# Three projections moved in a Perceiver-style kernel: queries' rows made by TensorE, late value products spread, a third chunk's values projected in the delta rule's front

## The chip, the cores and the metric

The kernel runs on one core of a Trainium2 chip. The core has five engines with queues of their own: TensorE (PE), VectorE (DVE), ScalarE (ACT), GpSimd (POOL) and SyncE (SP), which issues DMAs. They meet only through semaphores. PE writes to eight PSUM banks of 128 x 512 fp32, which DVE and ACT read. The metric is the device time in microseconds (us) of one execution.

## The reference

An input x of 128 rows x 256 passes through two layers; both attend to the same context of 12544 rows x 256.

```python
# layer 0: 4 heads of 64, softmax over 12544 context rows
x = x + softmax((ln(x) Wq)(ctx Wk)^T / 8) (ctx Wv) Wo
x = x + gated_delta_net(ln(x))        # 12 heads, 128 steps, short convolutions
x = x + moe(ln(x))                    # 8 experts, best 1
# layer 1: 16 heads of 16, softmax over the same context rows
x = x + softmax((ln(x) Wq' + bq)(ctx Wk' + bk)^T / 4) (ctx Wv' + bv)
x = x + gated_decay_attention(ln(x))
x = x + moe(ln(x))                    # 8 experts, best 2
```

## The kernel before

The context is cut into `NCH` = 14 chunks of 896 rows (seven tiles of 128). **Layer 0** streams them. DVE turns a chunk (`turn_context`, four steps T0 to T3), PE makes layer 0's keys (K0 to K3), layer 1's keys (J0 to J3) and both layers' values (V0 to V6, 512 columns: 256 for each layer), scores (S0 to S7), turned exponentials and value products. `PLAN0` is the order by hand; in a step chunk c's products stand between the projections of c + 1. Layer 1's keys go to DRAM (`kscr`) as six bf16 terms made by POOL, its values (`v1s`) to `vscr`. From chunk `LATE` = 12 on, layer 1's values are left out (256 columns); the turned context of these chunks stays in `ctxT0` and `ctxL`. A Fori loop runs steps 1 to 10. `PRO0` is the order of chunk 0's projections; in it "W0" turns the layer-1 weights (six DVE transposes, four on PE), which J0 needs.

**The delta rule** follows. Its front is serial: layer 0's output `o0`, its product with Wo, layer norm, gates, short convolutions, decay sums (`below`, L1194), norms (L1149). `spin` issues products of the identity whose results nobody reads. `vp` holds the products of the convolution taps.

**The experts**, then **layer 1**. `second_vector` splits the queries into three bf16 parts (`q3`). `qrows` needs them as 96 rows, six terms (`Q_TERM`) of 16 dimensions, heads side by side. SP writes `q3` to DRAM (`qscr`) and reads it back in six pieces. Then PE walks the prologue `PRO1`: 16 heads' scores of chunk 0, one of chunk 1, "M" (the turned running maximum, L1717), seven more of chunk 1. Two pairs of banks alternate, so a head's scores wait for the maximum (DVE, L1849) of the head two before. `late_values` makes the missing layer-1 values of chunks 12 and 13, five double units before the scores and two among them; ACT copies them to slots 1 and 2 of `v1`, SP stores them, and then fetches chunks 1 and 2 into these slots. POOL fills the three last rows of the keys (L1671, 3 x 12288 and 3 x 9216) and the matrix `blk16`, then takes up `maximum(c)`, whose result "M" turns. After that the chunks are streamed: transposed scores (L1752), exponentials (ACT), value products (L1765).

## Time and profile before

| what | value |
|---|---|
| runs | 1026.24, 1027.66, 1031.89 us (median 1027.66) |
| profiled execution | 1026.65 us, its span 1024.9 us, mean granted clock 0.99 |
| busy share of the span | PE 95%, weight loads 59%, ACT 52%, DVE 48%, POOL 29% |
| layer 0 / delta rule / experts | 0 to 517.7 / to 621.0 / to 638.3 us |
| layer 1's front / its streamed chunks | to 684.2 / to about 990 us |
| late values in layer 1's front | 28 products |

Times in the rows are microseconds from the span's start; a row of the timeline gives start, length, engine, line, operation, output and inputs with their form, the number of instructions, and in brackets the idle time before and who ended it. An fp32 product of PE counts as two records. A stage's limit is read from the brackets of the engine that is waited for.

### The profile page before, as it was taken

What the parts mean: (1) busy time and instruction counts of PE and PEld (TensorE: products, weight loads), DVE (VectorE), ACT (ScalarE), POOL (GpSimd) and SP (SyncE); (2) the same over time, 40 slices, a digit from 0 to 9 for tenths busy, and PEclk for the clock granted to TensorE, in tenths of its full rate; (3) what the DMA queues carried; (4) which work ended last, traced back from release to release, by engine and by line L of the source; (5) the groups of instructions that cost most, each with busy time, mean ns of one, the idle gap of its engine ahead of it and who ended that gap; (6) DMA issues with size and microseconds to landing.
All of it is one profiled execution on the core that took longest, in us unless ns stands there. A gap on an engine that the chain in (4) does not pass through costs nothing. (4 is left out here: it accounts for less than half of the span.)

```text
span 1024.9 us, 22398 instructions
## 1 busy us (share of the span) xinstructions
PE 973.8 (95%) x8646; PEld 608.7 (59%) x8646; DVE 494.1 (48%) x1002; ACT 535.8 (52%) x1243; POOL 301.8 (29%) x428
## 2 busy tenths in 40 slices
PE   8999999999999999999988998889999999999987
PEld 4445454554454554455577995647666666666775
DVE  3224233232332423333254453488878777887526
ACT  2544544454454454445547622226666666666753
POOL 5444253443344425344503611700100000010000
PEclk9999999999999999999999999989999999999999
DMA  9456646636546462552200005777657677765200
GB/s 157 159 154 189 184 169 181 156 116 135 130 160 171 126 186 104 124 151 108 76 34 1 2 1 151 178 214 226 154 151 182 171 172 185 183 157 151 86 3 5
DMA packets 106067, 136.88 MB, mean 134 GB/s; under 512 B 66568, under 2 KB 87840, under 8 KB 103296
## 3 DMA queue, kind: packets, MB, share of 16 engines
q1 hardware_dynamic: 102272, 134.81, 48.2%
q10 hardware_dynamic: 3712, 0.92, 0.6%
q8 instruction: 58, 0.95, 0.4%
q14 instruction: 25, 0.20, 0.1%
HBM read 81.88 MB, written 53.26 MB: 132 GB/s over the span
## 5 line engine op out<-in xcount | busy, mean ns | idle before, releaser
L1849 DVE TENSOR_REDUCE mx<-bank 128x1 f32<-128x896 f32 x224 | 233.8, 1086 | 62.3 <-PE bank L1709 58.9
L1910 ACT ACTIVATE p<-bank 128x512 f32<-128x512 f32 x392 | 204.0, 602 | 105.2 <-PE bank L1752 105.1
L549 PE MATMUL bank<-Wv,ctxT 128*128 128x512 f32 (+1 forms) x364 | 164.6, 587 | 0.0
L1752 PE MATMUL bank<-qrows,krows 99*128 99x128 bf16 x1568 | 124.4, 220 | 7.1 <-ACT p L1910 4.6
L1709 PE MATMUL bank<-krows,qrows 96*128 96x512 bf16 x448 | 125.3, 363 | 5.8 <-DVE mx L1849 4.8
L1752 PEld LDWEIGHTS bank<-qrows,krows 99*128 99x128 bf16 x1568 | 99.3, 97 | 44.5 <-issue 11.0
L618 DVE CUSTOM_DVE_ANT_0 sc<-bank,pen 128x448 f32<-128x448 f32 x112 | 65.7, 620 | 116.5 <-issue 116.5
L1765 PE MATMUL bank<-p,v 128*32 128x128 f32 x3136 | 108.4, 276 | 3.9 <-issue 3.9
L432 POOL CAST kt<-kf 128x512 bf16<-128x512 f32 (+1 forms) x56 | 31.1, 556 | 271.2 <-ACT kf L711 271.2
L1765 PEld LDWEIGHTS bank<-p,v 128*32 128x32 f32 x3136 | 80.6, 109 | 39.0 <-ACT p L1910 31.4
L549 PEld LDWEIGHTS bank<-Wv,ctxT 128*128 128x128 f32 x364 | 65.0, 190 | 64.2 <-issue 59.3
L529 PE MATMUL bank<-ctxT,WTk 128*128 128x512 f32 (+1 forms) x208 | 88.4, 547 | 1.0 <-ACT v L718 0.6
L1649 POOL TENSOR_SCALAR neg<-run 128x16 f32<-128x16 f32 x14 | 3.6, 255 | 274.5 <-DVE run L1864 274.5
L513 PE MATMUL bank<-ctxT,Wk 128*128 128x448 f32 x208 | 82.6, 540 | 1.2 <-issue 1.2
L726 ACT COPY v<-bank 128x256 f32<-128x256 f32 x84 | 31.1, 371 | 99.8 <-PE bank L549 99.8
L747 ACT COPY pT<-bank 128x512 f32<-128x512 f32 x98 | 56.6, 583 | 47.5 <-PE bank L560 47.4
L739 ACT ACTIVATE sc<-sc,neg 128x448 f32<-128x448 f32 x112 | 73.5, 663 | 0.2
L711 ACT ACTIVATE kf<-bank,b 128x512 f32<-128x512 f32 (+1 forms) x56 | 35.5, 634 | 69.7 <-PE bank L529 69.7
L560 PEld LDWEIGHTS bank<-ident,sc 128*128 128x128 f32 x392 | 42.8, 140 | 40.1 <-issue 32.5
L560 PE MATMUL bank<-ident,sc 128*128 128x128 f32 x392 | 62.3, 282 | 4.1 <-ACT pT L747 1.5
L644 DVE COPY ots<-bank 128x256 f32<-128x256 f32 x14 | 5.9, 425 | 124.5 <-PE bank L572 124.5
L434 POOL TENSOR_TENSOR kt<-kf,kt 128x512 bf16<-128x512 f32 (+1 forms) x56 | 61.4, 1096 | 4.5
(303 smaller groups left out, 1267.1 us busy)
## 6 DMA issues: line engine op xcount, KB each, us to landing
krows<-kscr SPq DMA_DIRECT2D x14, 1536.0 KB, 10.1
krows<-kscr SPq DMA_DIRECT2D x14, 1152.0 KB, 14.4
v<-vscr SPq DMA_DIRECT2D x14, 1004.5 KB, 12.7
vscr<-v1s SPq DMA_DIRECT2D x12, 1004.5 KB, 3.9
kscr<-kt SPq DMA_DIRECT2D x14, 768.0 KB, 3.6
kscr<-kt SPq DMA_DIRECT2D x14, 576.0 KB, 3.0
kscr<-kt SPq DMA_DIRECT2D x14, 512.0 KB, 4.5
ctxB<-ctx SPq DMA_DIRECT2D x56, 112.0 KB, 3.6
```

The lines of the kernel that those rows point to most:

```text
L434: pool.tensor_tensor(kh[:, 1, b], f, kh[:, 0, b], ALU.subtract).then_inc(S("k21"), 1)
L513: ins = pe.matmul(bank[kv_bank(op, s)][:, 0:HCH], Wk0[:, i, b * P:(b + 1) * P], turned_context(c)[:, i, half * HCH:(half + 1) * HCH], star ...
L529: ins = pe.matmul(bank[kv_bank(op, s)][:, 0:HW[half]], WTk[:, i, b * P:(b + 1) * P], turned_context(c)[:, i, HO[half]:HO[half] + HW[half]] ...
L549: ins = pe.matmul(bank[kv_bank(op, s)][:, 0:w * D], turned_context(c)[:, i, k * P:(k + 1) * P], Wv01[:, i, 0:w].rearrange("p w o -> p (w o)"),
L560: ins = pe.transpose(bank[PT[(s + t) % 2]][:, h * P:(h + 1) * P], sc0[:, s, h, t * P:(t + 1) * P], ident[:])
L618: dve.tensor_tensor_reduce(out=sc0[:, s, h, half * HCH:(half + 1) * HCH], in0=bank[SX[k % 2]][:, 0:HCH], in1=pen0[:, half * HCH:(half + 1) ...
L739: act.activation(sc0[:, s, h, cols], sc0[:, s, h, cols], ACT.Exp, bias=neg0[:, h:h + 1], accum_out=den0[:, s, h, half:half + 1]).then_inc( ...
L1709: ins = pe.matmul(bank[b + half][:, 0:HW[half]], qrows[0:KROWS, 0, h, :], krows[half][0:KROWS, r, krow(h), :], start=True, stop=True)
L1752: ins = pe.matmul(bank[ST1[g % 3]][:, i * P:(i + 1) * P], krows[half][:, c % R1, krow(h), cols], qrows[:, c % 2, h, :], start=True, stop=True)
L1765: ins = pe.matmul(bank[OT1][32 * i:32 * i + 32, j * P:(j + 1) * P], v1[:, c % R1, t, h * (D1 + 1):h * (D1 + 1) + 32], p1[:, g % PR, i * P: ...
L1849: dve.tensor_reduce(mx1[:, c % 2, h:h + 1], psum[:, b:b + 2, :].rearrange("p b n -> p (b n)")[:, 0:CH], AX.X, ALU.max).then_inc(S("smread1 ...
L1910: act.activation(p1[:, g % PR, :], bank[ST1[g % 3]][:], ACT.Exp).then_inc(S("exp1"), 1)
```

## The change

Chunk 11 joins the late chunks (`LATE` = 11). Chunk 12's turned context goes to `ctxM`, the upper part of `vpair`, a buffer that outlives layer 0 and serves as `v1s` before and as `vp` after. Its layer-1 values are made in the delta rule's front (`mid_values`, seven units of two products) and stored by SP; POOL clears `vp` after that. Chunks 11 and 13 are made in layer 1, 14 single units, one before the scores and 13 among them (`LAFTER`).

The queries' rows are made by PE: `picks` holds columns of the identity, written by POOL during the experts into `v1`'s slot 2; 24 products (`pick_rows`) give the 96 rows of 16 heads, and ACT copies them in four pieces. The gather of chunk 1's keys is issued ahead of that.

In layer 0's start SP waits for the first half of chunk 0's context ahead of the layer-1 weights, and "W0" stands behind the first two scores. The Fori loop runs steps 1 to 8, and 9 and 10 stand in straight code.

```diff
@@ -176,7 +176,7 @@
-        LATE = NCH - 2
+        LATE = NCH - 3
@@ -188,6 +188,7 @@
+        vpair = sb(gw, "vpair", [P, TAPS * 2 * GH * P])
@@ -250,7 +251,8 @@
-        v1s = sb(l0, "v1s", [P, 2, CT, VW])
+        v1s = vpair[:, 0:2 * CT * VW].rearrange("p (s t w) -> p s t w", s=2, t=CT)
+        ctxM = vpair[:, CT * VW:CT * VW + DC * CH].rearrange("p (i m) -> p i m", i=DC)
@@ -268,7 +270,7 @@
-        PRO0 = ALL0[0:8] + ("W0",) + ALL0[8:]
+        PRO0 = ALL0[0:10] + ("W0",) + ALL0[10:]
@@ -289,7 +291,9 @@
-            return ctxL if isinstance(c, int) and c == NCH - 1 else ctxT0
+            if isinstance(c, int) and c >= NCH - 2:
+                return ctxL if c == NCH - 1 else ctxM
+            return ctxT0
@@ -298,8 +302,10 @@
+                elif turned_context(c) is ctxL:
+                    dve.wait_ge(S("ctxT0"), 4 * c)
...
-                    dve.wait_ge(S("ctxT0"), 4 * c)
+                    dve.wait_ge(S("vscr_1"), 16 * (LATE // 2))
@@ -376,11 +382,11 @@
-            with eng.Fori(0, (NCH - 4) // 2) as i:
+            with eng.Fori(0, (NCH - 6) // 2) as i:
...
-            step(NCH - 3, 1, (NCH - 4) // 2)
-            step(NCH - 2, 0, (NCH - 2) // 2)
+            for c in range(NCH - 5, NCH - 1):
+                step(c, c % 2, c // 2)
@@ -463,6 +469,7 @@
+                sp.wait_ge(S("ctx0_0_0"), 64)
                 for k, name in ((1, "L1_xattn_Wk"), (2, "L1_xattn_Wv"), (0, "L1_xattn_Wq")):
@@ -824,16 +832,26 @@
+        MIDBANK = ((5, 0), (4, 0), (4, D), (5, 0), (7, 0), (7, D), (6, 0))
         def even_odd(tile, g):
...
         with nc.Block() as block:
+            @block.sync
+            def _(sp):
+                sp.wait_ge(S("v1mid"), CT)
+                sp.dma_start(vscr[NCH - 2].rearrange("p t w -> p (t w)"),
+                             v1s[:, 0].rearrange("p t w -> p (t w)")).then_inc(S("vscr_mid"), 16)
+                sp.wait_ge(S("vscr_mid"), 16)
             @block.gpsimd
...
+                pool.wait_ge(S("vscr_mid"), 16)
                 for j in range(TAPS - 1):
@@ -1046,8 +1064,18 @@
+                def take_mid(t, n):
+                    b, o = MIDBANK[t]
+                    act.wait_ge(S("v1mid_psum"), t + n)
+                    act.copy(v1s[:, 0, t:t + n, 0:H1 * (D1 + 1)].rearrange("p t (h d) -> p t h d", h=H1)[:, :, :, 0:D1],
+                             bank[b][:, o:o + n * D].rearrange("p (t h d) -> p t h d", t=n, h=H1)).then_inc(S("v1mid"), n)
+                take_mid(0, 1)
...
+                take_mid(1, 2)
+                take_mid(3, 1)
@@ -1060,6 +1088,9 @@
                 keep_rows(3)
+                act.activation(spare0[:], mhalf[:, 0:1], ACT.Silu)
+                take_mid(4, 2)
+                take_mid(6, 1)
                 silu(0, "conv", 1)
@@ -1169,7 +1200,20 @@
-                spin(pe, 5, 5)
+                def mid_values(t):
+                    b, o = MIDBANK[t]
+                    if t == 3:
+                        pe.wait_ge(S("v1mid"), 1)
+                    if t == 4:
+                        pe.wait_ge(S("gstep"), 1)
+                    for k in range(DC):
+                        ins = pe.matmul(bank[b][:, o:o + D], ctxM[:, k, t * P:(t + 1) * P], Wv01[:, k, 1, :],
+                                        start=(k == 0), stop=(k == DC - 1))
+                    ins.then_inc(S("v1mid_psum"), 1)
+                mid_values(0)
+                spin(pe, 4, 2)
                 pe.wait_ge(S("o0"), 1)
@@ -1179,9 +1223,10 @@
                 ins.then_inc(S("x1_psum"), 1)
-                spin(pe, 5, 11)
+                for t in range(1, 4):
+                    mid_values(t)
                 ln_pe(pe, "ln1", 7)
-                spin(pe, 5, 2)
+                spin(pe, 3, 2)
                 pe.wait_ge(S("ln1_hT"), 1)
@@ -1189,13 +1234,17 @@
                     project(g)
+                for t in range(4, CT):
+                    mid_values(t)
                 pe.wait_ge(S("R"), 1)
                 for g in range(NG):
+                    if g == 2:
+                        pe.wait_ge(S("v1mid"), CT)
                     pe.matmul(bank[DB[g]][:], below[:], R[:, hb(g)].rearrange("p h t -> p (h t)"), start=True,
...
                 pe.wait_ge(S("qcopy"), 2)
-                spin(pe, 2, 14)
+                spin(pe, 2, 5)
                 pe.wait_ge(S("sq"), 1)
@@ -1500,7 +1549,9 @@
-        qscr = nc.dram_tensor("qscr", (3, D, P), BF16).ap()
+        HB = P // D1
+        pickhome = v1[:, 2].rearrange("p t w -> p (t w)")[:, 0:3 * HB * KROWS // 2]
+        picks = pickhome.bitcast(BF16).rearrange("p (l k r) -> p l k r", l=HB, k=3)
@@ -1534,15 +1585,22 @@
...
+            value_ones(pool, 1)
+        def value_ones(pool, r):
+            pool.memset(v1[:, r, :, 0:H1 * (D1 + 1)].rearrange("p t (h d) -> p t h d", h=H1)[:, :, :, D1],
+                        1.0).then_inc(S("v1late_ones"), 1)
+            pool.memset(v1[:, r, :, H1 * (D1 + 1):], 0.0).then_inc(S("v1late_ones"), 1)
...
-        LU = 2 * CT // 2
-        LBANK = (4, 5)
+        LATES = (LATE, NCH - 1)
+        LU = 2 * CT
+        LBANK = (4, 5, 7)
+        LAFTER = (0, 1, 3, 4, 6, 7, 9, 10, 12, 13, 15, 18, 20)
+        LATE_FIRST = 1 + sum(1 for n in LAFTER if n <= H1 + 1)
+        NPICK = 4
+        PBANK = (3, 6, 7, 0)
@@ -1607,27 +1665,24 @@
-            sp.wait_ge(S("q3"), 3)
-            sp.dma_start(qscr.rearrange("k (b p) q -> p (k b) q", b=DC),
-                         q3[:].rearrange("p k b q -> p (k b) q")).then_inc(S("qscr"), 16)
-            sp.wait_ge(S("qscr"), 16)
-            for j in range(NJ):
-                sp.dma_start(qrows[j * D1:(j + 1) * D1, 0],
-                             qscr[Q_TERM[j]].rearrange("(h d) q -> d h q", d=D1)).then_inc(S("qrows_in"), 16)
-            sp.wait_ge(S("qrows_in"), 16 * NJ)
-            sp.dma_start(qrows[0:KROWS, 1], qrows[0:KROWS, 0]).then_inc(S("qrows_copy"), 16)
...
-            sp.wait_ge(S("v1late"), LU)
-            for r in (1, 2):
-                sp.dma_start(vscr[LATE + r - 1].rearrange("p t w -> p (t w)"),
-                             v1[:, r].rearrange("p t w -> p (t w)")).then_inc(S("vscr_late"), 16)
+            sp.wait_ge(S("qpicked"), NPICK)
+            sp.dma_start(qrows[0:KROWS, 1], qrows[0:KROWS, 0]).then_inc(S("qrows_copy"), 16)
+            def store_late(r):
+                sp.wait_ge(S("v1late"), r * CT)
+                sp.dma_start(vscr[LATES[r - 1]].rearrange("p t w -> p (t w)"),
+                             v1[:, r].rearrange("p t w -> p (t w)")).then_inc(S(f"vscr_late{r}"), 16)
+            store_late(1)
...
-            sp.wait_ge(S("vscr_late"), 32)
-            fetch_values(sp, 1)
-            fetch_values(sp, 2)
+            store_late(2)
+            for r in (1, 2):
+                sp.wait_ge(S(f"vscr_late{r}"), 16)
+                fetch_values(sp, r)
@@ -1641,6 +1696,15 @@
+        def make_picks(pool):
+            pool.wait_ge(S("moe0wt"), 1)
+            pool.memset(pickhome, 0.0).then_inc(S("picks"), 1)
+            pool.wait_ge(S("picks"), 1)
+            for j in range(NJ):
+                pool.tensor_copy(picks[:, :, Q_TERM[j], j * D1:(j + 1) * D1],
+                                 identb[:].rearrange("p (l d) -> p l d", d=D1)).then_inc(S("picks"), 1)
@@ -1665,7 +1729,11 @@
+            make_picks(pool)
             ln_pool(pool, "ln2")
+            pool.wait_ge(S("qpick_psum"), NPICK)
+            value_ones(pool, 2)
+            pool.wait_ge(S("v1late_ones"), 4)
             pool.wait_ge(S("q3"), 3)
@@ -1786,28 +1854,37 @@
...
-                for j in range(2):
-                    r, t = divmod(2 * i + j, CT)
-                    for k in range(DC):
-                        ins = pe.matmul(bank[b][:, j * D:(j + 1) * D], (ctxT0, ctxL)[r][:, k, t * P:(t + 1) * P],
-                                        Wv01[:, k, 1, :], start=(k == 0), stop=(k == DC - 1))
+                b = LBANK[i % 3]
+                if i >= 3:
+                    pe.wait_ge(S("v1late"), i - 2)
+                r, t = divmod(i, CT)
+                for k in range(DC):
+                    ins = pe.matmul(bank[b][:, 0:D], (ctxT0, ctxL)[r][:, k, t * P:(t + 1) * P],
+                                    Wv01[:, k, 1, :], start=(k == 0), stop=(k == DC - 1))
...
-            for i in range(LU - 2):
-                late_values(i)
-            pe.wait_ge(S("qrows_in"), 16 * NJ)
+            def pick_rows(i):
+                pe.wait_ge(S("lT"), (0, 1, 2, 3)[i])
+                for l in range(2):
+                    for k in range(3):
+                        ins = pe.matmul(bank[PBANK[i]][0:KROWS, l * D:(l + 1) * D], picks[:, 2 * i + l, k, :],
+                                        q3[:, k].rearrange("p b q -> p (b q)"), start=(k == 0), stop=(k == 2))
+                ins.then_inc(S("qpick_psum"), 1)
+            pe.wait_ge(S("picks"), NJ + 1)
+            pe.wait_ge(S("q3"), 3)
+            for i in range(NPICK):
+                pick_rows(i)
+            late_values(0)
...
+            pe.wait_ge(S("qpicked"), NPICK)
...
-                if n >= len(PRO1) - 6:
-                    spin(pe, OT1, 2)
-                if n in (3, 7):
-                    late_values(LU - 2 + n // 4)
+                if n in LAFTER:
+                    late_values(LAFTER.index(n) + 1)
+                elif n > len(PRO1) - 7:
+                    spin(pe, 6, 2)
@@ -1914,14 +1991,25 @@
-            act.wait_ge(S("v1late_ones"), 4)
-            for i in range(LU):
+            for i in range(NPICK):
+                act.wait_ge(S("qpick_psum"), i + 1)
+                act.copy(qrows[0:KROWS, 0].rearrange("r (b l) q -> r l b q", b=DC)[:, 2 * i:2 * i + 2],
+                         bank[PBANK[i]][0:KROWS].rearrange("r (l b q) -> r l b q", l=2, b=DC)).then_inc(S("qpicked"), 1)
+            def take_late(i):
+                if i % CT == 0:
+                    act.wait_ge(S("v1late_ones"), 2 * (i // CT) + 2)
+                act.copy(v1late[:, i, 0:H1 * (D1 + 1)].rearrange("p (h d) -> p h d", h=H1)[:, :, 0:D1],
+                         bank[LBANK[i % 3]][:, 0:D].rearrange("p (h d) -> p h d", h=H1)).then_inc(S("v1late"), 1)
+            for i in range(LATE_FIRST):
+                take_late(i)
...
+            for i in range(LATE_FIRST, LU):
+                take_late(i)
```

On DVE at the start (`gate` and `sc` belong to a head's scores) the rows before are:

```order
L345 TENSOR_SCALAR q<-bank 128x256
L663 TENSOR_SCALAR pen<-mask 128x896
L628 STREAM_TRANSPOSE WTk<-v 128x8x16 x2
L631 STREAM_TRANSPOSE Wv<-v 128x256
L628 STREAM_TRANSPOSE WTk<-v 128x8x16 x2
L631 STREAM_TRANSPOSE Wv<-v 128x256
L617 MEMSET gate 128x1
```

and after:

```order
L351 TENSOR_SCALAR q<-bank 128x256
L670 TENSOR_SCALAR pen<-mask 128x896
L624 MEMSET gate 128x1
L625 ISA sc,mx<-bank,pen 128x448
L625 ISA mx 128x1
L624 MEMSET gate 128x1
L625 ISA sc,mx<-bank,pen 128x448
L625 ISA mx 128x1
L635 STREAM_TRANSPOSE WTk<-v 128x8x16 x2
```

Two heads' scores have moved ahead of the six turns. On PE the delta rule's front stood before with spins around the products of `o` (layer 0's output), `xn` (the norm) and `Wc` (convolution inputs):

```order
L163 MATMUL bank<-ident 128x128 x5
L1175 MATMUL bank<-ident,o 128x128 x2
L1180 MATMUL bank<-Wo,oT 128x256 x2
L163 MATMUL bank<-ident 128x128 x11
L157 MATMUL bank<-ident,xn 128x128 x2
```

and stands after with value products of chunk 12 (`vpair`):

```order
L1211 MATMUL bank<-Wv,vpair 128x256 x2
L163 MATMUL bank<-ident 128x128 x2
L1219 MATMUL bank<-ident,o 128x128 x2
L1224 MATMUL bank<-Wo,oT 128x256 x2
L1211 MATMUL bank<-Wv,vpair 128x256 x6
L157 MATMUL bank<-ident,xn 128x128 x2
```

Fourteen of the spins have become four units of value products. On POOL in layer 1, before, the norm's root stood right ahead of the memsets of the keys' rows:

```order
L151 TENSOR_TENSOR rstd<-rstd,mhalf 128x1
L1671 MEMSET krows 3x12288
L1671 MEMSET krows 3x9216
L1674 MEMSET blk 128x128
L1677 AFFINE_SELECT blk<-blk 128x128
```

and after, the clearing of `v1`'s slot 2 (for which POOL waits on `qpick_psum`) stands between:

```order
L151 TENSOR_TENSOR rstd<-rstd,mhalf 128x1
L1591 MEMSET v 128x7x16
L1593 MEMSET v 128x7x15
L1739 MEMSET krows 3x12288
L1739 MEMSET krows 3x9216
L1742 MEMSET blk 128x128
```

The large memsets have moved behind the last product of the picks.

## Rows read from the trace of the kernel before

**Rows 1.** The page, part 5: an ACT copy of one bank

```profile
L747 ACT COPY pT<-bank 128x512 f32<-128x512 f32 x98 | 56.6, 583 | 47.5 <-PE bank L560 47.4
```

**Rows 2.** Timeline, DVE: layer 0's copies (start us, us, engine, line, operation, [idle before])

```profile
403.82 0.42 DVE L644 COPY ots<-bank 128x256 f32<-128x256 f32 x1 [9.48 <-PE bank L572]
...
440.26 0.42 DVE L644 COPY ots<-bank 128x256 f32<-128x256 f32 x1 [9.37 <-PE bank L572]
...
472.65 0.42 DVE L644 COPY ots<-bank 128x256 f32<-128x256 f32 x1 [6.02 <-PE bank L572]
...
504.11 0.42 DVE L644 COPY ots<-bank 128x256 f32<-128x256 f32 x1 [6.01 <-PE bank L572]
```

**Rows 3.** Timeline of the start: context, weight turns, scores, first product J0

```profile
13.04 1.17 DVE L304 STREAM_TRANSPOSE ctxT<-ctxA 128x448 f32<-128x448 f32 x2 [3.81 <-DMA ctxA<-ctx]
...
14.31 3.25 PE L513 MATMUL bank<-ctxT,Wk 128*128 128x448 f32 x8 [1.20 <-issue]
...
15.31 0.65 DVE L628 STREAM_TRANSPOSE WTk<-v 128x128 f32<-128x128 f32 x2 [0.27 <-DMA v<-L_xattn_Wq]
...
16.58 0.41 DVE L631 STREAM_TRANSPOSE Wv<-v 128x256 f32<-128x256 f32 x1
...
17.92 1.02 PE L540 MATMUL bank<-kT,q 64*128 64x448 f32 x4
...
18.88 1.98 PE L529 MATMUL bank<-ctxT,WTk 128*128 128x512 f32 x4
...
18.98 0.62 DVE L618 CUSTOM_DVE_ANT_0 sc<-bank,pen 128x448 f32<-128x448 f32 x1 [1.99 <-issue]
```

**Rows 4.** Timeline of the delta rule's front, PE

```profile
520.93 2.62 PE L163 MATMUL bank<-ident 128*128 128x128 f32 x22
...
533.63 3.29 PE L163 MATMUL bank<-ident 128*128 128x128 f32 x28
...
537.46 1.50 PE L1149 MATMUL bank<-half,sq 128*128 128x2 f32 x12 [0.54 <-DVE sq L926]
```

**Rows 5.** Timeline of layer 1's front, PE, DVE and POOL

```profile
645.21 6.21 PE L1797 MATMUL bank<-Wv,ctxT 128*128 128x256 f32 x28
...
645.67 18.16 POOL L1671 MEMSET krows<- 3x12288 f32 x2 [5.11 <-DVE q L1843]
...
654.81 0.93 PE L1709 MATMUL bank<-krows,qrows 96*128 96x512 bf16 x4 [0.79 <-DMA qrows<-qscr]
...
655.49 4.20 DVE L1849 TENSOR_REDUCE mx<-bank 128x1 f32<-128x896 f32 x4 [9.95 <-PE bank L1709]
...
658.36 2.80 PE L1797 MATMUL bank<-Wv,ctxA 128*128 128x256 f32 x8
...
661.58 4.08 DVE L1849 TENSOR_REDUCE mx<-bank 128x1 f32<-128x896 f32 x4 [1.88 <-PE bank L1709]
...
664.60 0.34 POOL L1680 TENSOR_SCALAR_AFFINE_SELECT blk<-blk 128x128 f32<-128x128 f32 x1
...
672.67 0.93 PE L1709 MATMUL bank<-krows,qrows 96*128 96x512 bf16 x2 [0.19 <-DVE mx L1849]
...
674.76 0.17 DVE L1864 TENSOR_TENSOR run<-run,mx 128x16 f32<-128x16 f32 x1
...
676.51 0.34 PE L1717 MATMUL bank<-identb,n 128*96 128x128 bf16 x1 [1.85 <-POOL n L1661]
...
684.20 0.84 PE L1752 MATMUL bank<-qrows,krows 99*128 99x128 bf16 x12
```

**Rows 6.** Windows: PE busy, granted clock, DMA share, GB/s

```profile
657.00:658.00 1.00, 0.83 (x3) 0.50 1.10 377
...
674.00:675.00 1.00, 0.66 (x2) 0.50 0.06 24
```

**Rows 7.** DMA issues, 626 to 631: KB each, us to landing

```profile
krows<-kscr SPq DMA_DIRECT2D x1, 1536.0 KB, 15.7
krows<-kscr SPq DMA_DIRECT2D x1, 1152.0 KB, 19.9
```

18 lines of the change are left out of this document (4 added, 14 removed).

## The prediction

> **What bounds the kernel now.** I read the page first: TensorE (PE) is busy 95% of the span, but in stages with different limits. I cut the time into stages with the timeline and, inside each, looked at what ends PE's idle time.
>
> In layer 0 the DVE copy that closes a chunk's value product marks the period. The last three gaps are 36.44, 32.39 and 31.46 us [rows 2]. The reader should see that the periods get shorter exactly where a chunk is built without the second half of its value product, so what PE streams there is the bound.
>
> The first chunk's prologue is a mixture. DVE waits 3.81 us for the second half of the context and starts turning it at 13.04; PE starts the key products for it at 14.31, the first scores at 17.92 and the first product J0 at 18.88 [rows 3].
>
> The front of the delta rule is a serial chain through DVE, ACT and POOL. PE fills its waits with empty products (spins) there: 22 and 28 records [rows 4].
>
> The front of layer 1 has two limits in a row. First the round trip of the queries through DRAM: the first scores start at 654.81 with "DMA qrows<-qscr" as releaser. Then DVE's maxima, 1.05 us each (4.20 for four), 24 of them in the prologue, with pauses of which the one at 661.58 (1.88 us, released by PE) is the largest [rows 5]. The streamed chunks after 684.20 do not change.
>
> **The change part by part.** The sum is made against the profiled execution: span 1024.9, its own time 1026.65, which is 1.0 below the median shown (1027.66).
>
> *Layer 0, chunk 11 without the layer-1 half.* Fourteen products get 256 instead of 512 columns, ACT loses seven copies, and SP one store. No need to price them singly: the steps that build chunks 12 and 13 in this way are in the trace. Before, the last three gaps add to 36.44 + 32.39 + 31.46 = 100.29; after, the first short gap moves one chunk forward and a second 31.46 follows: 32.39 + 31.46 + 31.46 = 95.31. Gain 5.0. Bounds: 4.0 (36.44 - 32.39, if the added step got nothing beyond the first short one) to 6.0 (fourteen times the 0.43 that 256 fp32 columns cost, two records of 0.222 each, 6.21 for 28 [rows 5]). Chunk 12's turning no longer waits for chunk 11's last product, but PE was not waiting for it, so that is 0. Two more steps out of the loop are 0 as well: the gap that lies in straight code differs from the looped ones only by its work.
>
> *The start.* Three loads of layer-1 weights now wait until the first half of chunk 0's context is in, and DVE and PE take the first two scores before they turn those weights. The second half of the context should come earlier: DVE was waiting for it since about 9.2, and it shared the DMA with these loads. If it is turned by 13.1, where PE ends the first key products, the second key products start 1.2 earlier, at 13.1. They last 3.25, so the scores start at 16.4. DVE takes them 1.06 after PE begins (17.92 to 18.98), needs 1.17 for two, and only then turns the weights, which took from 15.31 to 16.99 = 1.68. J0 needs all six turns: 16.4 + 1.06 + 1.17 + 1.68 + 0.2 = 20.5 against 18.88 [rows 3]. What was hidden under the wait for the context is now in the chain: a loss of 1.6. Bounds: 2.9 if the context comes no earlier, 0.5 if PE starts the chunk 1.1 earlier too. Behind J0 the prologue is PE's, so the loss is kept.
>
> *Delta rule.* Seven units of two products, 0.89 us each (four records of 0.222, rows 5), 6.2 in all; 23 spins go, 46 records of about 0.118 [rows 4], 5.4. Units 0 to 3 take the places of 14 spins in waits for DVE and POOL. Units 4 to 6 (2.7) stand before the decay sums, and nine spins fewer (2.1) behind them; the next norm product at 537.46 waits for DVE either way. I take 0.15 lost. ACT's four copies fall in its waits, the Silu table is loaded where it was. The new 1 MB store is waited for by POOL alone, whose next work is at 547. If that cover were gone the price would be the whole 6.2; below, it could gain nothing, since spins are not on the path.
>
> *Layer 1, queries by PE.* The qscr write, six reads and the wait go. Instead PE makes 24 bf16 products of 256 columns; no such row exists. The nearest is the bf16 score pair: four matmuls, 1792 columns, in 0.93, so 0.13 for 256 and 3.2 for all; from above, 0.222 each like an fp32 record, 5.3; from below, 2.6, if they run a fifth faster than that pair. I take 3.2. The queries' last part is there when POOL starts at 645.67, so the products end at 648.9; ACT's last copy takes 0.58 [rows 1]; the scores start at 649.5 instead of 654.81. POOL makes the picking tables before, in its idle time during the experts; the first late unit fits beside ACT's copy.
>
> *The score prologue.* The late products (14 units instead of 7 double ones) are spread: PE needs per three heads 3 x 0.46 (half of 0.93) + 2 x 0.89 = 3.16, DVE 3 x 1.05 = 3.15. That is even, with no reserve. I give it 0.5 of friction. First maximum at 650.2, sixteen end at 650.2 + 16.8 + 0.5 = 667.5, against 674.76 [rows 5]. That would be 7.3 earlier.
>
> *But POOL is late next.* Its 18.16 us of memsets on the key rows' tail started at 645.67. Now they stand behind the last pick product and two small memsets, at about 649.5, and end at 667.7; the block matrix behind them ended 1.1 later (664.94 for 663.83), so POOL is free at 668.8, 1.3 after the maximum. From the running maximum to the product that turns it (L1717) are 1.75; from POOL's start 1.5. It comes at 670.3 instead of 676.51: 6.2 earlier. Behind it, 7.69 passed until the streamed scores (684.20). Two late units now stand there in place of two spins: at half clock 1.40 instead of 0.94 each (8 records in 2.80, rows 5; a spin pair is four records of 0.235), so about 1.0 more. Streamed scores at 679.0: gain 5.2. Bounds: 2.5 with PE slower throughout that stretch, 9 if neither POOL nor the clock costs anything and the picks are quick.
>
> GpSimd's work beside DVE has a rule. DVE's maxima take 1.05 each beside POOL's memset (655.49) [rows 5]. The Trainium skill, GPSIMD Engine Reference, section Key points, says that GpSimd shares its SBUF interfaces with VectorE and contends with instructions that have two SBUF inputs. By it, the picks would slow the experts' last DVE steps by up to their own length, some 2 us; no run here shows them, and the sum with them would be 1020.5.
>
> *Sum:* -5.0 + 1.6 + 0.15 - 5.2 = -8.45. 1026.65 - 8.45 = 1018.2; a median that lies a little above a single run makes it 1018.5.
>
> **Rivals.**
> 1. *Nothing else is late* (POOL's memsets and the clock cost nothing). The front gains 8 to 9, the upper bound above: 1015. For it: DVE alone set the pace. Against it: POOL's row is 18.16 long and starts later by construction.
> 2. *PE stays at half clock behind the running maximum.* PE has no work there from about 666.9 to 670.3. The granted clock was 0.50 at 657 and again at 674, each time after PE had done little for some us [rows 6]. Then seven score pairs of 0.93, two late units of 1.40 and four spin pairs of 0.94 make 13.1, against the 8.7 used above: 4.4 more, 1023.
> The Trainium skill (TensorE: Matmul & The Clock Gate, section HAM oscillation) describes this: a gap in PE's work gives the slow clock at the next burst. The trace agrees with the direction.
> 3. *The keys come later, so nothing starts earlier.* Chunk 1's keys are now asked for right behind chunk 0's values. Chunk 0's keys landed 15.7 and 19.9 after their issue at 626.1 and 626.7, so at 646.6, only 2.9 before they are wanted [rows 7]. If both gathers share the engines instead of following one another, 2.65 MB at the same rate (11 us for that size) push it to 657.6 and the front's gain is gone, and more: 1018.5 + 8.1 = 1026.6. Against it: the landings before follow the order of issue.
> 4. *Slower: the spread value products at half clock.* Place: the prologue from the first score to the streamed ones. Price: 24 pairs of 0.93 + 13 units of 1.40 + four spin pairs of 0.94 = 44.3, against 29.5 (649.5 to 679.0): 14.8 more, 1033.3. It decides as soon as the granted clock reads 0.50 for most of 650 to 666; it breaks even with before when it holds for some 60% of it. For it: balance without reserve, and before it fell to half at 657. Against: that followed a wait which is removed, and at full clock PE is never idle for long.
>
> **How the numbers follow.** Forecast 0.56, rival 1 0.14, rival 2 0.15, rival 3 0.08, rival 4 0.05; 0.02 for anything else, slower. The forecast's own range is 1016 to 1021 (terms: start +-1.2, layer 0 +-0.7, front +-1.8). For 8 in 10 I take in rival 1 and rival 2: 1013.5 to 1023.5. A measurement of this kernel tells about 0.5% (5.1 us) from no change, so faster means below 1022.5. Forecast nearly whole, rival 1 and a third of rival 2 are faster: 0.78. Same: two thirds of rival 2, most of rival 3: 0.16. Slower 0.06.
>
> **What the profile after would show.** Layer 0: the copies' last three gaps 32.4, 31.5, 31.5. Start: J0 about 1.6 later, DVE's weight turns behind two scores, and the second context half landing by 11. Delta: the norm product at the same distance from the block's start within 0.3. Layer 1, counted from the first transposes of lraw at 643.03: first scores after 6.5 instead of 11.8; no pause over 0.5 in the first sixteen maxima; POOL's first running-maximum step released by POOL's own work, not by DVE; streamed scores after 36 instead of 41.2. I am wrong if the first scores have a DMA as releaser, if PE's clock reads 0.50 before the sixteenth maximum, if delta grows by more than 1, or if J0 is not later.

## The result and the profile after

| | before | after |
|---|---|---|
| first comparison, median | 1028.38 us (1026.24 to 1031.89, 4 runs) | 1017.33 us (1016.64 to 1017.38, 4 runs) |
| with the runs made beside the experiments | 1028.8 us (1023.7 to 1036.4, 47 runs) | 1016.7 us (1013.1 to 1018.3, 10 runs) |
| profiled execution, its span | 1026.65, 1024.9 | 1017.3, 1015.5 |

The ratio of the first comparison is 0.988, 95% interval 0.9858 to 0.9902. The forecast was 1018.5. It was 9.2 us below the median of 1027.66 that was known then; the medians of the first row differ by 11.0 us, those of the second by 12.1. So the gain was forecast 2 to 3 us too small, while the time itself came out near.

In layer 0 these are the DVE copies that close a chunk's value product, now on line L651 (timeline, DVE). Their gaps are 32.32, 31.46 and 31.47, where before they were 36.44, 32.39 and 31.46 [rows 2].

```profile
404.32 0.42 DVE L651 COPY ots<-bank 128x256 f32<-128x256 f32 x1 [9.37 <-PE bank L579]
436.64 0.42 DVE L651 COPY ots<-bank 128x256 f32<-128x256 f32 x1 [6.02 <-PE bank L579]
468.10 0.42 DVE L651 COPY ots<-bank 128x256 f32<-128x256 f32 x1 [6.02 <-PE bank L579]
499.57 0.42 DVE L651 COPY ots<-bank 128x256 f32<-128x256 f32 x1 [6.02 <-PE bank L579]
```

At the start (timeline, DVE and PE) the second half of the context comes at 10.89 instead of 13.04 and the key products run unbroken. Then J0 (L536) waits 2.40 us for the weight turn on L638, which stands behind two scores, and starts at 19.44 instead of 18.88 [rows 3]. DVE had been idle for 3.52 us ahead of the first score.

```profile
9.33 6.18 PE L520 MATMUL bank<-ctxT,Wk 128*128 128x448 f32 x16
10.89 1.17 DVE L310 STREAM_TRANSPOSE ctxT<-ctxA 128x448 f32<-128x448 f32 x2 [2.12 <-DMA ctxA<-ctx]
15.44 1.02 PE L547 MATMUL bank<-kT,q 64*128 64x448 f32 x4
16.58 0.06 DVE L624 MEMSET gate<- 128x1 f32 x1 [3.52 <-PE bank L547]
18.98 0.41 DVE L638 STREAM_TRANSPOSE Wv<-v 128x256 f32<-128x256 f32 x1
19.44 1.98 PE L536 MATMUL bank<-ctxT,WTk 128*128 128x512 f32 x4 [2.40 <-DVE Wv L638]
```

In the front of the delta rule (timeline, PE) value products (L1211) stand where the empty products stood [rows 4]. The norm product (L1180) comes 19.33 us behind the block's first DVE instruction (513.24 to 532.57; before 517.78 to 537.46, 19.68).

```profile
516.43 2.75 PE L1211 MATMUL bank<-Wv,vpair 128*128 128x256 f32 x12
...
526.16 2.75 PE L1211 MATMUL bank<-Wv,vpair 128*128 128x256 f32 x12
...
531.33 1.28 PE L163 MATMUL bank<-ident 128*128 128x128 f32 x10
532.57 1.50 PE L1180 MATMUL bank<-half,sq 128*128 128x2 f32 x12
```

In layer 1's front (timeline, all engines) the 24 pick products take 2.79, ACT's four copies end at 642.5, and yet the first scores (L1777) wait 1.95 for the keys of chunk 0. Against [rows 5] the scores come 8.23 behind the transposes of lraw (L1852) instead of 11.78, the last update of the running maximum (L1941) 19.31 behind them instead of 19.95, and the streamed scores (L1820) 8.64 behind the turned maximum (L1785) instead of 7.69.

```profile
636.44 2.35 PE L1852 MATMUL bank<-ident,lraw 128*128 128x128 f32 x20
639.06 2.79 PE L1871 MATMUL bank<-q,v 128*96 128x256 bf16 x24 [0.27 <-issue]
639.92 2.55 ACT L1996 CAST qrows<-bank 96x512 bf16<-96x512 f32 x4 [0.30 <-PE bank L1871]
642.41 10.33 POOL L1739 MEMSET krows<- 3x12288 f32 x1
644.67 0.54 PE L1777 MATMUL bank<-krows,qrows 96*128 96x512 bf16 x2 [1.95 <-DMA krows<-kscr]
645.34 1.09 DVE L1926 TENSOR_REDUCE mx<-bank 128x1 f32<-128x896 f32 x1 [6.38 <-PE bank L1777]
647.01 1.09 DVE L1926 TENSOR_REDUCE mx<-bank 128x1 f32<-128x896 f32 x1 [0.58 <-PE bank L1777]
649.41 3.09 DVE L1926 TENSOR_REDUCE mx<-bank 128x1 f32<-128x896 f32 x3 [1.31 <-PE bank L1777]
...
663.98 0.17 DVE L1941 TENSOR_TENSOR run<-run,mx 128x16 f32<-128x16 f32 x1
664.25 0.28 POOL L1713 TENSOR_SCALAR neg<-run 128x16 f32<-128x16 f32 x1 [2.56 <-DVE run L1941]
665.74 0.26 PE L1785 MATMUL bank<-identb,n 128*96 128x128 bf16 x1 [2.10 <-POOL n L1725]
...
674.38 0.84 PE L1820 MATMUL bank<-qrows,krows 99*128 99x128 bf16 x12
```

The granted clock (windows: PE busy, clock, DMA share, GB/s) is 0.50 in two places of that stretch, where it was so at 657 and about 674 before [rows 6]. It is full in the experts.

```profile
621.00:625.00 4.00, 3.92 (x21) 1.00 0.63 192
646.00:649.00 3.00, 3.00 (x9) 0.50 0.95 175
667.00:669.00 2.00, 2.00 (x7) 0.50 0.04 6
```

The experts were not part of the forecast, and they took 14.94 us after and 16.69 before. One product of four records there shows the difference. The first row is from the trace before, the second from the one after:

```profile
627.47 2.88 PE L1326 MATMUL bank<-p,hT 128*128 128x512 f32 x4
```

```profile
621.55 1.88 PE L1375 MATMUL bank<-p,hT 128*128 128x512 f32 x4
```

By stage, from one trace of each: start +0.56, layer 0 behind J0 -5.11, front of the delta rule -0.34, experts -1.75, layer 1 from lraw to the streamed scores -3.23 (41.17 to 37.94), streamed chunks and the end +0.42. That is -9.45, and the spans differ by 9.4. Three of these terms were not forecast in that size: the experts (nothing forecast), the front (-5.2) and the start (+1.6). Their errors cancel in part, so the sum came near the forecast partly by luck. The experiments ask which terms hold in every execution.

### The profile page after: what moved, and what is told of

Read it like the earlier page. It is cut to its first block and busy times, and to the rows that moved or that the text cites. A ratio compares the mean times of both kernels' runs of the same rounds, so it can differ in the third digit from the quotient of the medians.

```text
span 1015.5 us, 22296 instructions
## 1 busy us (share of the span) xinstructions
PE 966.8 (95%) x8648; PEld 609.8 (60%) x8648; DVE 494.1 (49%) x1002; ACT 540.1 (53%) x1253; POOL 304.6 (30%) x435
## 5 line engine op out<-in xcount | busy, mean ns | idle before, releaser
L556 PE MATMUL bank<-Wv,ctxT 128*128 128x512 f32 (+1 forms) x336 | 151.4, 586 | 0.0
L1820 PE MATMUL bank<-qrows,krows 99*128 99x128 bf16 x1568 | 124.6, 220 | 9.3 <-ACT p L1987 4.6
L1820 PEld LDWEIGHTS bank<-qrows,krows 99*128 99x128 bf16 x1568 | 99.2, 97 | 46.4 <-issue 13.1
L1777 PE MATMUL bank<-krows,qrows 96*128 96x512 bf16 x448 | 123.6, 357 | 3.4 <-DMA krows<-kscr 2.0
L556 PEld LDWEIGHTS bank<-Wv,ctxT 128*128 128x128 f32 x336 | 60.0, 190 | 59.1 <-issue 54.5
L536 PE MATMUL bank<-ctxT,WTk 128*128 128x512 f32 (+1 forms) x192 | 81.6, 547 | 3.4 <-DVE Wv L638 2.4
L733 ACT COPY v<-bank 128x256 f32<-128x256 f32 x77 | 28.5, 371 | 91.4 <-PE bank L556 91.4
L520 PE MATMUL bank<-ctxT,Wk 128*128 128x448 f32 x192 | 76.0, 539 | 0.0
L651 DVE COPY ots<-bank 128x256 f32<-128x256 f32 x14 | 5.9, 425 | 121.0 <-PE bank L579 121.0
```

Of the source, the lines that this page charges most:

```text
L520: ins = pe.matmul(bank[kv_bank(op, s)][:, 0:HCH], Wk0[:, i, b * P:(b + 1) * P], turned_context(c)[:, i, half * HCH:(half + 1) * HCH], star ...
L536: ins = pe.matmul(bank[kv_bank(op, s)][:, 0:HW[half]], WTk[:, i, b * P:(b + 1) * P], turned_context(c)[:, i, HO[half]:HO[half] + HW[half]] ...
L556: ins = pe.matmul(bank[kv_bank(op, s)][:, 0:w * D], turned_context(c)[:, i, k * P:(k + 1) * P], Wv01[:, i, 0:w].rearrange("p w o -> p (w o)"),
L1777: ins = pe.matmul(bank[b + half][:, 0:HW[half]], qrows[0:KROWS, 0, h, :], krows[half][0:KROWS, r, krow(h), :], start=True, stop=True)
L1820: ins = pe.matmul(bank[ST1[g % 3]][:, i * P:(i + 1) * P], krows[half][:, c % R1, krow(h), cols], qrows[:, c % 2, h, :], start=True, stop=True)
```

## The experiments

Ten edited kernels ran, and the two of the comparison once more; each also gave a trace. The table has what all traces say of the same stretches, each read from the starts of the timeline's rows. "Last copy" is the last DVE copy of layer 0, "experts" goes to their bias product, "maximum" the last update of the running maximum, "turned" the product that turns it, "streamed" the first transposed scores. The column "half" adds, over one-microsecond windows, twice what the granted clock lacks to 1.00: the time at half clock. A constant 5.3 us between that product and the transposes of lraw is left out.

| kernel | J0 at | to last copy | to experts | experts | lraw to scores | to maximum | to turned | to streamed | to end | half | span |
|---|---|---|---|---|---|---|---|---|---|---|---|
| before | 18.88 | 497.09 | 105.05 | 16.69 | 11.78 | 19.95 | 1.75 | 7.69 | 340.7 | 20.5 | 1024.9 |
| before_again | 18.61 | 497.09 | 105.07 | 16.69 | 11.77 | 20.11 | 1.75 | 7.76 | 342.0 | 21.0 | 1026.2 |
| after | 19.44 | 491.98 | 104.73 | 14.94 | 8.23 | 19.31 | 1.76 | 8.64 | 341.1 | 10.8 | 1015.5 |
| after_again | 20.05 | 493.58 | 103.08 | 16.33 | 6.13 | 17.64 | 3.05 | 8.64 | 340.9 | 13.7 | 1014.7 |
| e_gather_behind | 19.84 | 491.95 | 104.70 | 14.94 | 6.13 | 17.63 | 3.06 | 8.43 | 339.7 | 10.3 | 1011.7 |
| e_keys_first | 19.46 | 493.56 | 104.70 | 15.31 | 6.66 | 17.64 | 3.06 | 9.65 | 340.1 | 13.6 | 1015.5 |
| e_start_undone | 17.82 | 491.97 | 103.08 | 16.69 | 6.13 | 17.63 | 3.07 | 8.64 | 339.5 | 6.8 | 1009.9 |
| e_wait_only | 17.34 | 491.96 | 104.68 | 16.32 | 6.12 | 17.64 | 3.05 | 8.64 | 340.4 | 13.6 | 1011.5 |
| e_wait_pool | 17.29 | 491.96 | 103.09 | 14.94 | 6.13 | 17.63 | 1.76 | 8.64 | 341.3 | 4.3 | 1008.1 |
| e_wait_pool_spins | 17.22 | 491.96 | 103.09 | 16.33 | 6.13 | 17.64 | 2.61 | 6.94 | 339.5 | 6.8 | 1006.8 |
| e_mid_spins | 19.81 | 493.57 | 106.26 | 14.94 | 6.13 | 17.64 | 3.05 | 9.94 | 344.5 | 20.5 | 1021.2 |
| e_round_trip | 19.74 | 493.62 | 103.09 | 18.74 | 22.60 | 20.42 | 1.76 | 8.64 | 340.2 | 41.0 | 1034.2 |
| e_round_trip_behind | 19.90 | 493.65 | 104.72 | 14.94 | 15.14 | 19.86 | 1.75 | 8.63 | 339.0 | 23.9 | 1023.0 |
| e_layer0_only | 18.65 | 491.96 | 103.08 | 18.71 | 10.82 | 18.71 | 1.75 | 7.61 | 340.8 | 23.9 | 1017.5 |

**The changed kernel again, no edit.**

> The changed kernel once more, as a second trace of it beside the experiments. The first trace waited 1.95 us for chunk 0's keys (they landed 22.8 us after their issue) ahead of the first scores; in three other kernels with the same front they landed after 19.6 to 21.8 and nothing waited. Theory A (that wait is a matter of the single execution): here the first scores come 6.1 us after lraw's first transposes, the 16th maximum's update 17.6 later, POOL's step is then late and the turned maximum 3.06 behind it, the streamed scores 8.6 behind that: 35.5 in all against 37.9, and the times spread down to 1013.5. Theory B (the wait is there in most executions of this kernel): 37.9 again, and six times within 1 us of 1017.3.

Measured: median 1016.05 (1013.08 to 1018.28, 6 runs). Theory A holds. The timeline shows what the forecast had described. Nothing waits for keys, and POOL has its memsets behind it only after the maximum has been updated, so its step starts by its own work:

```profile
644.51 0.54 PE L1777 MATMUL bank<-krows,qrows 96*128 96x512 bf16 x2
645.18 2.24 DVE L1926 TENSOR_REDUCE mx<-bank 128x1 f32<-128x896 f32 x2 [4.29 <-PE bank L1777]
...
662.15 0.18 DVE L1941 TENSOR_TENSOR run<-run,mx 128x16 f32<-128x16 f32 x1
...
663.29 0.34 POOL L1748 TENSOR_SCALAR_AFFINE_SELECT blk<-blk 128x128 f32<-128x128 f32 x1
663.72 0.28 POOL L1713 TENSOR_SCALAR neg<-run 128x16 f32<-128x16 f32 x1
```

The column "lraw to scores" says the same of the whole set: 6.12 to 6.13 in seven of the nine traces with the products by PE, 6.66 in one, and 8.23 in the first trace of the changed kernel alone.

**Chunk 1's keys asked for behind the copy of the picked rows.**

```diff
-            gather(sp, 1, 0)
-            gather(sp, 1, 1)
             sp.wait_ge(S("qpicked"), NPICK)
             sp.dma_start(qrows[0:KROWS, 1], qrows[0:KROWS, 0])...
+            gather(sp, 1, 0)
+            gather(sp, 1, 1)
```

> The changed kernel with one edit: SP asks for chunk 1's keys behind the copy of the picked query rows, as the kernel before did behind its round trip, and not right behind chunk 0's values. Theory (chunk 0's keys were late because chunk 1's share the DMA engines with them): chunk 0's keys land within 20 us of their issue, the first scores come 6.5 us after the first transposes of lraw instead of 8.2 and are released by ACT's last pick copy, the granted clock does not fall to 0.50 at the first maxima, the 16th maximum ends 1.7 to 3 us earlier; POOL's memsets are then what is late by up to 1.3, so the whole time falls by 1 to 3 us, to 1014.5 to 1016.5. Rival (chunk 0's keys are late because they are issued late and read 2.7 MB behind 1.3 MB of weights, whoever is behind them): the first scores stay at 8.2, and chunk 1's keys, asked for 16 us later, may now be late for the 17th score: 1017 to 1020.

Measured: median 1017.16 (1013.45 to 1017.61, 6 runs), no difference from the changed kernel (+0.5, 95% interval -2.2 to 1.8). The trace has the first scores at 6.13, about what the theory asked for (6.5), but after_again has that too, without the edit. The landings decide (DMA issues of the second half of chunk 0's keys: KB, us from issue to landing). First the changed kernel's first trace, then this kernel's:

```profile
krows<-kscr SPq DMA_DIRECT2D x1, 1152.0 KB, 22.8
```

```profile
krows<-kscr SPq DMA_DIRECT2D x1, 1152.0 KB, 20.7
```

With chunk 1's keys queued behind them, these keys took 19.5 to 21.8 in seven traces and 22.8 in the first trace of the changed kernel; with chunk 1's keys asked for later they took 18.9 to 21.6 in five traces (19.9 before [rows 7], 20.7 here). The two ranges overlap, so sharing is not shown to be what made them late, and the 20 us that the theory named were not reached even here. In seven of the eight traces with the products by PE and the keys in this place they landed 0.2 to 2.8 us ahead of the first scores, in one 2.0 behind the time at which these would have started (after: 644.53 for 642.57).

How much time they have depends on the experts' clock. From their issue to the first scores at 6.13 there are 20.9 us where the experts took 14.94, and 22.3 to 22.6 where these ran partly at half clock. The first trace had both at once: fast experts and the slowest landing. Why that landing took 22.8 stays open.

**Chunk 0's keys ahead of lraw.**

```diff
         def l1_loads(sp):
+            gather(sp, 0, 0)
+            gather(sp, 0, 1)
             o = (0, 6, 8, 10)
...
-            gather(sp, 0, 0)
-            gather(sp, 0, 1)
```

> The changed kernel with one edit: chunk 0's keys are asked for ahead of the layer's weights (lraw, decays, biases), not behind them; chunk 1's stay right behind chunk 0's values. Theory (the keys' landing is a matter of what shares the DMA engines with them): the keys land some 5 us earlier, the first scores come 6.5 us after lraw's first transposes, no half clock at the first maxima; 1.5 to 3 us less, if lraw is still there when its transposes want it. Rival: 2.7 MB ahead of lraw push lraw behind its first transposes (it landed 4.9 us after its issue in the trace before, and is wanted some 15 us behind it); then the transposes start later by 1 to 5 us and the time is 1018 to 1022.

Measured: median 1016.93 (1015.67 to 1026.17, 6 runs): no gain. The keys landed 9.3 and 13.9 us after their issue, so that part held. The last piece of lraw now took 17.1 (5.4 before the edit) and landed just ahead of the first transposes. The first scores came at 6.66 and not earlier than the 6.13 of the others, so what the edit gave was a reserve that these executions did not need.

**The start: order undone, wait kept.**

```diff
-        PRO0 = ALL0[0:10] + ("W0",) + ALL0[10:]
+        PRO0 = ALL0[0:8] + ("W0",) + ALL0[8:]
```

> The changed kernel with one edit: DVE and PE turn layer 1's weights ahead of all scores again, as before; the three weight loads still wait for the first half of chunk 0's context. Theory A (of the start's two edits only the order costs, since the weight turns lie between the second score and J0 while DVE idled 3.5 us ahead of the first score): the turns fit in that idle time, J0 comes at 17.7 to 18.2 instead of 19.44, and the whole time falls by 1.3 to 1.7 to about 1015.8. Theory B (the weights, asked for 1 us later and sharing the engines with the second half of the context, are not there before about 17): DVE waits for them ahead of the first score, J0 comes at 19.5 to 20.5, and the time is 1017.3 to 1018.5.

Measured: median 1012.44 (1009.10 to 1014.69, 6 runs), 4.2 below the changed kernel (95% interval from resampling the runs 1.7 to 6.7), against before 0.983 (0.980 to 0.986). The six runs of after_again have 0.9873 (0.9852 to 0.9895) against before. Theory A had the mechanism. J0 came at 17.34, a little earlier than its 17.7 to 18.2, and the gain is larger than the 1.3 to 1.7 that it said. DVE waits 1.40 us for the weights and has turned them all when PE is done with the keys (timeline):

```profile
14.96 0.65 DVE L635 STREAM_TRANSPOSE WTk<-v 128x128 f32<-128x128 f32 x2 [1.40 <-DMA v<-L_xattn_Wq]
...
16.24 0.41 DVE L638 STREAM_TRANSPOSE Wv<-v 128x256 f32<-128x256 f32 x1
...
17.34 1.98 PE L536 MATMUL bank<-ctxT,WTk 128*128 128x512 f32 x4
```

The table has the rest. With the new order J0 came at 19.44 to 20.05, in the middle 19.81 (seven traces); with the old order and no wait at 17.82 to 18.88, middle 18.63 (four); with the old order and the wait at 17.22 to 17.34 (three). And in five of the seven traces with the new order layer 0 took 1.6 us more behind J0 (493.6 for 492.0), in none of the others. There the clock fell right behind J0's wait (after_again, timeline and windows; J0's four records took 2.74 instead of 1.98):

```profile
20.05 2.74 PE L536 MATMUL bank<-ctxT,WTk 128*128 128x512 f32 x4 [2.39 <-DVE Wv L638]
```

```profile
21.00:22.00 1.00, 1.00 (x3) 0.57 1.36 204
22.00:23.00 1.00, 1.00 (x3) 0.50 1.09 196
```

So by the traces the order costs 19.81 - 17.29 = 2.5 by itself (17.29 is the middle of the three) and 1.6 x 5/7 = 1.1 through the clock, 3.6 together, beside the 4.2 of the medians. Why the clock fell behind the same wait of 2.4 us in five traces and not in the other two (after and e_gather_behind), no run shows.

**The start: both edits undone.**

```diff
-                sp.wait_ge(S("ctx0_0_0"), 64)
-        PRO0 = ALL0[0:10] + ("W0",) + ALL0[10:]
+        PRO0 = ALL0[0:8] + ("W0",) + ALL0[8:]
```

> The changed kernel with both edits of the start undone (no wait ahead of the three weight loads, the weights turned ahead of all scores), all else as changed. By the comparison of the two traces the start cost 0.56 us, so J0 comes at 18.9 again and the time is 1016.7; a rival is that the loads of later weights, moved by the wait, mattered elsewhere in layer 0: then it differs by more than 1 from 1017.3 in either direction.

Measured: median 1015.24 (1011.64 to 1021.29, 6 runs), 1.4 below the changed kernel, interval -4.1 to 3.1: by time alone undecided. J0 came at 17.82 here, where 18.9 was expected, and at 18.65 in e_layer0_only, which starts in the same way. Behind J0 layer 0 took 491.97, as it did with the wait kept (491.96), so the trace has nothing for the rival.

**POOL's memsets in another order**, on top of e_wait_only.

```diff
-            pool.wait_ge(S("qpick_psum"), NPICK)
-            value_ones(pool, 2)
-            pool.wait_ge(S("v1late_ones"), 4)
             pool.wait_ge(S("q3"), 3)
             for half in range(2):
                 pool.memset(krows[half][KROWS:KONES]...)
                 pool.wait_ge(S("krows_ones"), half + 1)
+                if half == 0:
+                    pool.wait_ge(S("qpick_psum"), NPICK)
+                    value_ones(pool, 2)
+                    pool.wait_ge(S("v1late_ones"), 4)
```

> The kernel of e_wait_only (weights turned ahead of all scores, the three weight loads still waiting) with one more edit: POOL fills the first half of the key rows' tail ahead of its wait for the last pick product and the two small memsets, instead of behind them. Theory (behind the running maximum POOL is the one that is late, since its step came 1.57 us after the maximum's last update in e_wait_only's trace, 3.05 us from that update to the turned maximum against 1.75 before): the step follows the update at once, the turned maximum comes 1.75 behind it, and the whole time falls by 1.3 to about 1011.1. Rival: PE then has the same work in a shorter stretch and the next wait takes the gain (ACT's copies of the late values, or the keys of chunk 1): the streamed scores come no earlier, 1012.4.

Measured: median 1012.16 (1008.15 to 1016.42, 6 runs). In the trace the step is as the theory has it: released by DVE, the maximum turned 1.76 behind its update instead of 3.05, the streamed scores 34.16 behind lraw instead of 35.45. That is the 1.3 by which POOL was late. In time it can't be told from e_wait_only (-0.3, interval -4.1 to 3.5).

```profile
635.27 10.33 POOL L1736 MEMSET krows<- 3x12288 f32 x1 [5.11 <-DVE q L1921]
```

```profile
656.66 0.28 POOL L1713 TENSOR_SCALAR neg<-run 128x16 f32<-128x16 f32 x1 [1.67 <-DVE run L1942]
```

**Empty products in that wait**, on top of e_wait_pool.

```diff
             for n, op in enumerate(PRO1):
+                if op == ("M", 0, 0):
+                    spin(pe, 6, 14)
                 side(*op)
```

> The kernel of e_wait_pool with 14 empty products (1.65 us at full clock) ahead of the product that turns the first running maximum, where PE waits 2.10 us for POOL. In all traces with this front the granted clock falls to 0.50 behind that wait, and the streamed scores come 8.4 to 8.64 us behind the turned maximum. Theory (the clock falls for that idle time): it stays at 1.00, the stretch shrinks to about 7.2 and the whole by 1.4 on average, to about 1010.8. Rival (the fall has another cause, or DVE's maxima, 1.05 us each, set that stretch and not PE's clock): the clock or the 8.6 stay, and the time is 1012.2 or, if the spins delay the turned maximum, up to 0.3 more.

Measured: median 1012.61 (1008.58 to 1014.09, 6 runs). The expectation priced an empty product at one record; it is two, so the 14 took 3.29 us and the turned maximum came 2.61 behind the update, 0.85 later than without them. The clock stayed full, and from there to the streamed scores it took 6.94 instead of 8.64 (the other traces with this front have 8.43 to 9.94, a wider range than the expectation gave). The theory on the clock holds in this one trace, against eight others without the empty products in which the clock fell there. The net gain in the trace is 0.85; the medians do not show it (+0.5, interval -3.4 to 3.6).

```profile
657.20 3.29 PE L163 MATMUL bank<-ident 128*128 128x128 f32 x28
```

```profile
657.00:663.00 6.00, 6.00 (x46) 1.00 0.05 20
```

**Empty products for chunk 12's values** (these values are left out).

```diff
-                mid_values(0)
-                spin(pe, 4, 2)
+                spin(pe, 5, 5)
...
-                for t in range(4, CT):
-                    mid_values(t)
...
-                spin(pe, 2, 5)
+                spin(pe, 2, 14)
```

> The changed kernel without the seven units that project chunk 12's layer-1 values in the front of the delta rule (that chunk's layer-1 values are left out, so it computes less); the empty products of the kernel before stand in their places, and ACT's four copies go; the store is kept. In the traces the block from its first DVE instruction to the norm product took 19.34 us with the units and 19.68 with the empty products. Theory A (the units are wholly covered and the 0.34 is not theirs): norm product 19.3 to 19.7 behind the block's start, the whole within 0.5 us of 1017.3. Theory B (units that fill PE let the product's end be seen sooner than empty ones): 0.3 to 0.4 later here, again at Wo's product: 1.64 from its start to DVE's sum instead of 1.23. Theory C (they cost something that another difference hides): 0.5 to 1 earlier.

Measured: median 1019.45 (1014.41 to 1022.93, 6 runs). The norm product came 19.29 behind the block's start (515.20 to 534.49), and from Wo's product to DVE's sum it took 1.24, as with the value products: theory A for this stretch; the whole time, which it put within 0.5 of 1017.3, missed. The 0.4 that before took longer there (1.64, in both of its traces) has another cause, which no run here tells. The median is 2.8 above the changed kernel (interval -0.6 to 5.0) though the kernel computes less. Its trace was half-clocked at one more place, right behind the norms (to the experts 106.26), and its end took 344.5, where the others took 339 to 342. The latter stays open.

**The queries through DRAM again**, chunk 1's keys left ahead of the round trip. The picks, PE's products with them and ACT's copies go.

```diff
-            sp.wait_ge(S("qpicked"), NPICK)
+            sp.wait_ge(S("q3"), 3)
+            sp.dma_start(qscr..., q3...).then_inc(S("qscr"), 16)
+            sp.wait_ge(S("qscr"), 16)
+            for j in range(NJ):
+                sp.dma_start(qrows[j * D1:(j + 1) * D1, 0], qscr[Q_TERM[j]]...)
+            sp.wait_ge(S("qrows_in"), 16 * NJ)
```

> The changed kernel with the queries' rows fetched through DRAM again (one write, six reads) in place of the products by PE; the late value products stay spread between the scores. Theory (the products are what brought the first scores forward): the first scores come 11.8 us after lraw's first transposes, released by the DMA, 5.7 later than with the products; the granted clock falls to 0.50 behind that wait, since PE has no late products to fill it; the streamed scores come 40 to 42 after lraw, as in the kernel before (41.2), so the whole is 1019.5 to 1021.5. Rival (the gain came from spreading the late products and DVE's earlier start is given back at POOL): the stretch from the first scores on is shorter by the 1.3 us for which POOL was late, and the whole is within 1.5 us of 1017.3.

Measured: median 1037.27 (1034.01 to 1040.43, 6 runs), slower than before: 1.0088 (1.0064 to 1.0112). Both expectations missed by over 15 us. The write of 192 KB landed 14.7 us after its issue, since it stood behind 2.7 MB of chunk 1's keys; PE had nothing to do for 18.9 us and ran at half clock behind it.

```profile
qscr<-q SPq DMA_DIRECT2D x1, 192.0 KB, 14.7
```

```profile
650.00:656.00 6.00, 0.00 (x0) 0.50 0.67 164
...
662.00:668.00 6.00, 4.82 (x12) 0.50 0.22 66
```

**The same with chunk 1's keys behind it.** The gather stands behind the copy, as in the diff of e_gather_behind.

> As e_round_trip (the queries' rows through DRAM, late value products spread), with chunk 1's keys asked for behind the round trip and the copy, as in the kernel before, and not ahead of it. In e_round_trip the first scores came 22.6 us behind lraw's first transposes and the whole took 1037.3. Theory (that was the small write and reads standing behind 2.7 MB of chunk 1's keys on SP's queue; what the products by PE buy is the round trip itself): first scores 11.8 behind lraw as before, streamed scores 40 to 42 behind it, the whole 1019.5 to 1021.5. Rival (the keys' place in the queue is not what matters, the spread late products leave PE idle and at half clock in the wait): the first scores at 11.8 to 13, but the time is 1025 or more.

Measured: median 1025.43 (1019.24 to 1029.40, 12 runs); first scores 15.14 behind lraw. The write landed after 7.2, where it took 3.9 and 4.1 in the two traces before; that is the 3.4 by which the first scores come later than there. Neither statement is met whole. Of the 10.8 us by which 22.6 exceeds the 11.8 of before, the queue made 7.5; but the first scores come later than either statement has them, and at 1025.4 the rival's bound on the time is reached. Spreading the late products also takes away the work with which PE filled the round trip (ten of the 14 units stood ahead of the scores then), and the clock is at 0.50 from 648 to 656. From e_gather_behind this kernel differs only in how the queries' rows are made, so the products by PE are worth 8.3 us of the medians (1025.43 to 1017.16, interval 7.1 to 11.8) beside spread late products.

```profile
648.00:652.00 4.00, 0.00 (x0) 0.50 0.41 91
652.00:656.00 4.00, 2.27 (x6) 0.50 0.33 74
```

**Layer 0's part alone**: e_round_trip_behind with the start undone and ten of the 14 late units ahead of the scores.

```diff
-            late_values(0)
+            for i in range(10):
+                late_values(i)
...
-                if n in LAFTER:
-                    late_values(LAFTER.index(n) + 1)
-                elif n > len(PRO1) - 7:
-                    spin(pe, 6, 2)
+                if n >= len(PRO1) - 6:
+                    spin(pe, OT1, 2)
+                if n in (3, 7):
+                    late_values(10 + n // 2 - 1)
+                    late_values(11 + n // 2 - 1)
```

> The kernel before with one part of the change alone: chunk 11's layer-1 values late and chunk 12's in the front of the delta rule. The start is undone, the queries' rows go through DRAM with chunk 1's keys behind them, and the late values (14 units of one product pair, ten ahead of the scores, four between them) stand as before. Theory (the terms add): layer 0's end comes 5.05 us earlier, the block of the delta rule takes as long as before, and from lraw's first transposes to the streamed scores it is 41 us as before: 1028.7 - 5.1 = 1023.6. Rival (the terms do not add, since stretches at half clock move with the phase of the program): layer 0 is 5.05 shorter all the same, but the whole differs from 1023.6 by more than 2.

Measured: median 1021.37 (1018.92 to 1025.36, 10 runs); against before 0.9924 (0.9898 to 0.995). Layer 0 behind J0 is 5.13 shorter (497.09 to 491.96). The rest of the 7.4 between the medians lies in stretches which vary by 1.6 to 2 with the clock (the trace has 103.08 for 105.05 in the delta rule, and 18.71 for 16.69 in the experts), and in a front of 38.9 instead of 41.2 to 41.4. So this front is not quite that of before: the late values are made in single units, and the write of the queries landed in 2.3 us (3.9 before). The median differs from 1023.6 by 2.2, just past the rival's bound of 2, but the interval of the ratio is 2.7 us wide to either side: the times do not decide between the two.

**The kernel before again, no edit.**

> The kernel before once more, for a second trace of it. In the first its granted clock was 0.50 at four places, 20.5 us in all counted as half clock, against 10.8 and 13.7 in the two traces of the changed kernel. Theory (the clock falls at about the same places in every execution: behind the experts' start, behind the round trip, and for long behind the running maximum): again 17 us or more in all, the longest spell behind the running maximum, 670 to 681. Rival (the places are chance): the long spell is gone or elsewhere, and from the turned maximum to the streamed scores it takes less than 7.69.

Measured: 1028.0, once. 21.0 us at half clock for 20.5, the long stretch again at 670 to 681, 7.76 for 7.69. The theory holds for this kernel; in the changed one the places differ between its two traces. The front of before (timeline, PE) goes with it: in [rows 5] and here PE waits for DVE's maxima time after time (0.45, 0.19), since most late products were used up ahead of the scores. In the first trace before, at 670, where the long stretch begins, PE had been busy for 0.43 to 0.56 of each microsecond since 667.

```profile
669.47 0.55 PE L1709 MATMUL bank<-krows,qrows 96*128 96x512 bf16 x2 [0.45 <-DVE mx L1849]
...
672.58 0.93 PE L1709 MATMUL bank<-krows,qrows 96*128 96x512 bf16 x2 [0.19 <-DVE mx L1849]
```

## Why the prediction was right, point by point

**Layer 0, -5.0.** Right: -5.1 behind J0, in every trace in which the clock did not fall there, and -3.5 in the five in which it did.

**The start, +1.6.** Right in kind, with two errors that partly cancel. The term was too large: the new order put J0 1.2 later than without both edits (19.81 for 18.63). The chain from the first scores to J0 was priced at 4.1 and took 4.0; but the scores began at 15.44 and not at 16.4, because the second half of the context, turned at 10.89, was there before PE had finished with the first. And I took the loss to stay as it is. In five of seven traces PE's wait of 2.4 us ahead of J0 was followed by half clock, 1.6 more. I had looked for the clock in layer 1 alone.

**The delta rule, +0.15.** The norm product came 0.34 earlier, not later; e_mid_spins has 19.29 with empty products, so the units themselves cost nothing to within 0.05. They are covered, as argued.

**Queries by PE, scores at 6.5.** Right: 6.13 in most traces. The products took 2.79, where 3.2 was taken and the bound below was 2.6. The first trace after had 8.23, and by the test that I had set ("I am wrong if the first scores have a DMA as releaser") this step failed there. So it did by the next sign: behind that wait the clock read 0.50 from 646 to 649, before the sixteenth maximum, and the maxima had pauses of 0.58 and 1.31 us where none over 0.5 was forecast. In after_again neither happened. Rival 3 had foreseen the late keys, by sharing with chunk 1's. The wait is real, and sharing is not shown as its cause: the landing times without it lie in the same range.

**The prologue, 16.8 + 0.5 behind the first maximum.** 16.97 in after_again (645.18 to 662.15), so the friction is 0.2. With the spread products PE was busy and at full clock through the maxima (rival 4 did not happen):

```profile
646.00:656.00 10.00, 9.80 (x48) 1.00 0.96 230
```

**POOL late next.** Right wherever the keys were there in time: 3.05 from the update to the turned maximum instead of 1.75, which is the 1.3 forecast, and moving the memsets took it away (1.76). In the first trace the keys' wait of 1.95 was longer, and it hid POOL's.

**Streamed scores 8.7 behind the turned maximum.** 8.64. The half clock in that stretch, rival 2's mechanism, is in every trace but e_wait_pool_spins; the two late units at the slower rate already stood in the sum. Its own price of 13.1 was too high: it assumed half clock to the end, and the windows of after have it back at 1.00 from about 670.

**36 from lraw to the streamed scores.** 35.46 in after_again, 37.94 in the first trace, for 41.2. The gain of 5.2 was 5.7 and 3.2.

**GpSimd beside DVE.** The Trainium skill (GPSIMD Engine Reference, Key points) has it contend with VectorE's instructions of two SBUF inputs. Nothing of the size of 2 us is there: while POOL made the picks (624.41 to 627.02 in the first trace after), DVE's step on L1514 took 1.00 for two instructions, as the same step did without the picks before. Apart from a weight for each row, these instructions read one tensor from a bank and one from SBUF, so the rule's case of two SBUF inputs is hardly tested here. The experts took 14.94 at their shortest both with the picks and without them (e_round_trip_behind).

**What was not seen:** that the experts and the middle of the delta rule vary by 1.6 to 3.8 us with the clock. The experts' 1.75 in the first comparison is of that kind. It is not shown to be chance alone: the two stretches together took 121.7 in both traces before and 118.0 to 121.2 in all nine with the products by PE. On average these are 2 us less that the sum did not have, though PE's work in them is not less; it is part of why the gain was forecast too small.

What the change as a whole bought can be put so: layer 0's part alone 7.4 of the 12.1 between the medians (its own clean term is 5.1). The new start and the spread products, without the products by PE, lose 4.1 of it (1025.4 for 1021.4). The products by PE with chunk 1's keys ahead bring 8.7 (1025.4 to 1016.7). The start's order costs 3.6 by the traces and 4.2 by the medians, and the best kernels here stand at 1012.2 to 1012.6.

## What to carry over

Moves can depend on each other. With the round trip in place, putting large gathers ahead of it cost 11.8 us of the medians (1037.27 for 1025.43). The front with the spread products was 6.5 us longer there than without (45.38 for 38.89 from lraw to the streamed scores, e_round_trip_behind and e_layer0_only), but 4.3 of that lie ahead of the first scores, where the write of the queries landed 4.9 later, and that is not shown to be the spreading's doing. Whether the products by PE would have gained as much without the spreading was not run. A wait may cost more than its own length, for behind it PE was often at half clock here; real work in its place, or empty work as in e_wait_pool_spins, kept the clock full. And read at least two traces before explaining a stage by 2 us; the first one here showed a wait for keys and hid one for POOL, and the second showed the opposite.

## What the hardware showed unexpectedly

- The spread among executions goes with the time at half clock. Over 43 runs of the kernel before, the five with a mean granted clock of 0.992 or more took 1023.7 to 1028.0 us, and the eight with 0.987 or less took 1030.6 to 1036.4. Two traces of one kernel had it in different stages (after: delta rule; after_again: start and experts).
- A write of 192 KB landed in 2.3 to 4.1 us with little ahead of it on the same queue, in 7.2 and 14.7 behind larger reads. The copy of 384 KB took 3.8 to 4.6 with chunk 1's keys behind it and 9.0 to 18.1 with them ahead and not yet landed. That it cost nothing because chunk 1's scores came after it is argued, not tested.
- Issue itself can be held up: with 2.7 MB of keys ahead, SP's issue of one piece of lraw took 6.21 us instead of 0.47 (e_keys_first; after).
